# Query norms in a fused attention and feed-forward kernel: four small transfers in place of a TensorE transpose

## The reference

```python
q = (hidden_states @ Wq).reshape(B, Sq, H, D)            # B 4, Sq 512, H 16, D 128
k = (encoder_hidden_states @ Wk).reshape(B, Skv, H, D)
v = (encoder_hidden_states @ Wv).reshape(B, Skv, H, D)
q = rmsnorm(q, gq)                                       # x * rsqrt(mean(x^2) + eps) * g
k = rmsnorm(k, gk)
scores = jnp.einsum('bqhd,bkhd->bhqk', q, k) * scale
attn = jax.nn.softmax(scores, axis=-1)
out = jnp.einsum('bhqk,bkhd->bqhd', attn, v)
return out.reshape(B, Sq, H * D) @ Wo
...
x = x + jnp.tanh(g_xattn[0]) * _L0_xattn_ref(ctx_1024, _layernorm(x), ...)   # selective scan, the mixer
x = x + jnp.tanh(g_ffn[0]) * _L0_ffn_ref(_layernorm(x), ...)                 # quantized feed-forward
x = x + jnp.tanh(g_xattn[1]) * _L1_xattn_ref(_layernorm(x), ctx_1024, ...)   # the attention above
x = x + jnp.tanh(g_ffn[1]) * _L1_ffn_ref(_layernorm(x), ...)                 # four experts
```

## Time and profile before

| | |
|---|---|
| median of 3 runs | 1851.22 us |
| lowest, highest | 1843.35, 1852.04 us |
| time of the profiled execution | 1852.26 us |
| its span, first to last instruction | 1850.5 us |
| busy TensorE, DVE, ScalarE, POOL | 95%, 70%, 52%, 36% of the span |
| mean granted TensorE clock | 0.983 of full |

### The profile page before, as it was taken

How to read it: one execution, slowest core, us unless ns; L and a number is a source line. 1 busy time by engine, 2 the same in 40 slices (tenths; PEclk the granted TensorE clock), 3 DMA queues, 4 the chain that set the end, 5 groups by cost and what they waited for, 6 DMA issues and landing times.

```text
span 1850.5 us, 19507 instructions
## 1 busy us (share of the span) xinstructions
PE 1763.2 (95%) x6114; PEld 809.9 (44%) x6114; DVE 1300.1 (70%) x1899; ACT 963.8 (52%) x1920; POOL 666.5 (36%) x696
## 2 busy tenths in 40 slices
PE   8999899879999999999999999999999899999999
PEld 4333344334444444444444444444444344445543
DVE  4989686989998689899787998987652444422221
ACT  7988786446545546566455566555435334320100
POOL 2434322337463324557222564562223333310000
PEclk9999899979999999999999999999999999999999
DMA  7999833767851146897212589732112799837110
GB/s 262 242 289 286 244 109 116 203 164 187 199 142 57 51 100 162 208 240 200 66 30 74 156 188 251 199 95 69 35 57 91 218 282 293 236 119 273 40 51 28
DMA packets 159045, 292.11 MB, mean 158 GB/s; under 512 B 18424, under 2 KB 51704, under 8 KB 156000
## 3 DMA queue, kind: packets, MB, share of 16 engines
q1 hardware_dynamic: 141664, 227.95, 39.0%
q0 software_dynamic: 17280, 62.92, 17.5%
HBM read 169.51 MB, written 58.26 MB: 123 GB/s over the span
## 4 chain that ended last, share of the span: by engine, by line
PE 72%; DVE 13%; ACT 6%; issue 4%; DMA 3%; POOL 1%; SPq 1%; DVEq 0%; ACTq 0%; POOLq 0%
PE p L846 11%; PE p L806 10%; PE p L823 9%; PE p L857 8%; PE p L893 6%; PE p L697 5%; DVE s_M L1025 5%; PE p L780 4%; PE p L829 4%; PE p L908 3%; PE p L746 3%; PE p L785 3%; DVE s_M L1020 2%; DVE s_M L1032 1%; DVE s_U L1178 1%
## 5 line engine op out<-in xcount | busy, mean ns | idle before, releaser
L1025 DVE TENSOR_TENSOR_SCAN s_M<-s_M 128x1024 f32<-128x1024 f32 x128 | 296.4, 2315 | 9.9 <-ACT s_M L1290 7.6
L1178 DVE CUSTOM_DVE_ANT_0 s_U<-p,s_U 128x512 f32<-128x512 f32 x256 | 188.2, 745 | 161.0 <-PE p L823 159.7
L823 PE MATMUL p<-s_U 128*128 128x512 f32 x512 | 268.2, 612 | 4.6 <-DVE s_U L1178 3.0
L806 PE MATMUL p<-s_U 128*128 128x512 f32 x512 | 256.7, 610 | 3.4 <-ACT s_U L1418 2.7
L1534 POOL DMA_DIRECT2D s_u<-s_M x120 | 111.7, 931 | 383.7 <-DVE s_M L1032 355.6
L1579 POOL TENSOR_SCALAR s_U<-s_U 128x512 f32<-128x512 f32 x256 | 231.9, 926 | 6.3
L857 PE MATMUL p<-s_U 128*128 128x512 f32 x512 | 223.7, 593 | 0.0
L846 PE MATMUL p<-s_U 128*128 128x512 f32 x472 | 216.0, 599 | 2.5 <-ACT s_U L1431 2.4
L1431 ACT COPY s_U<-p 128x512 f32<-128x512 f32 x196 | 105.5, 594 | 176.3 <-PE p L829 175.0
L1290 ACT ACTIVATE s_M<-s_dl,s_small 128x511 f32<-128x511 f32 x256 | 170.3, 717 | 35.5 <-DVE s_M L1025 35.3
L1426 ACT ACTIVATE s_U<-s_U 128x512 f32<-128x512 f32 x256 | 181.6, 710 | 5.3
(11 more groups left out here) (194 smaller groups left out, 2458.3 us busy)
## 6 DMA issues: line engine op xcount, KB each, us to landing
s_u<-s_M POOLq DMA_DIRECT2D x120, 512.0 KB, 7.6
s_bc<-bc_scratch SPq DMA_DIRECT2D x96, 256.0 KB, 4.5
k_scratch<-s_U SPq DMA_DIRECT2D x16, 1024.0 KB, 7.9
v_scratch<-s_U SPq DMA_DIRECT2D x16, 1024.0 KB, 5.4
s_U<-in_Wq SPq DMA_DIRECT2D x64, 256.0 KB, 6.6
s_U<-k_scratch SPq DMA_DIRECT2D x64, 256.0 KB, 5.4
s_U<-rk_scratch SPq DMA_DIRECT2D x64, 256.0 KB, 5.8
s_U<-in_Wo SPq DMA_DIRECT2D x64, 256.0 KB, 4.5
```

The source lines that it names most:

```text
L806: ins = e.matmul(banks[bk][:], wqq[j % 2][:, k, :], axT[b % 2][:, k, :], start=(k == 0), stop=(k == 3))
L823: e.matmul(banks[bk][:], qT[j % 3][:, k * 128:(k + 1) * 128], kT[j % 2], start=True, stop=True).then_inc(S["a_s"], 1)
L1025: e.tensor_tensor_scan(w, dA[i % 2], w, 0.0, ALU.mult, ALU.add).then_inc(S["m_s"], 1)
L1178: e.tensor_tensor_reduce(out=Pm[j % 2][:, k, :], in0=banks[ABANK[kind, j, k]][:], in1=rkb[j % 2], scale=rq[:, k:k + 1], scalar=-3.0e38, op ...
```

## The change

The squares are written in another order: token p of chunk t goes to column 4p + t, not 128t + p. The four matmuls with ones are as before, so partitions 32g to 32g+31 now hold the sums of tokens 32g to 32g+31 of every chunk. One row of each group, cut in 32 pieces of four numbers, is what the partitions 32g to 32g+31 of `rq` need. SP moves it with four transfers, one for each group, to a new semaphore `d_nq`, and POOL's `power` waits for that. The TensorE transpose and the ScalarE copy of step `nt` are gone. ScalarE's next write of `nqs` waits for the transfers of the head before. The planner's cost for `nt` is changed, so the orders of all engines may change.

```diff
-    if x[0] in ("q", "nq", "nt"):
+    if x[0] in ("q", "nq"):
         ABANK[x] = 3
...
-"nt": [("PE", 0.2), ("ACT", 0.3), ("POOL", 1.1)]
+"nt": [("DMA", 2.5), ("POOL", 1.3)]
...
-                    elif kind == "nt":
-                        e.transpose(banks[bk][:, 128:256], nqs[:], identf[:]).then_inc(S["a_nt"], 1)
-                        freed[bk] = (S["a_nqv"], j + 1)
...
-                        e.activation(sq, banks[bk][:], ACT.Square).then_inc(S["a_qs"], 1)
+                        e.activation(sq.rearrange("d (p t) -> d t p", t=4), banks[bk][:].rearrange("d (t p) -> d t p", t=4), ACT.Square).then_inc(S["a_qs"], 1)
                     elif kind == "nq":
                         e.wait_ge(S["a_nq"], j + 1)
                         if j:
-                            e.wait_ge(S["a_nt"], j)
+                            e.wait_ge(S["d_nq"], 64 * j)
                         e.activation(nqs[:], banks[ABANK[kind, j, k]][:, 0:128], ACT.Copy, bias=EPS, scale=1.0 / HD).then_inc(S["a_nqs"], 1)
-                    elif kind == "nt":
-                        e.wait_ge(S["a_nt"], j + 1)
-                        if j >= 3:
-                            e.wait_ge(S["a_mx"], 4 * (j - 3) + 4)
-                        e.copy(rq, banks[ABANK[kind, j, k]][:, 128:256].rearrange("p (t c) -> p t c", c=32)[:, :, 0]).then_inc(S["a_nqv"], 1)
...
                     if kind == "nt":
-                        power(rq, (S["a_nqv"], j + 1), "a_rq")
+                        power(rq, (S["d_nq"], 64 * (j + 1)), "a_rq")
...
+                    elif kind == "nt":
+                        e.wait_ge(S["a_nqs"], j + 1)
+                        if j >= 3:
+                            e.wait_ge(S["a_mx"], 4 * (j - 3) + 4)
+                        for g in range(4):
+                            e.dma_start(head_stats(j)[4][32 * g:32 * g + 32, :],
+                                        nqs[32 * g:32 * g + 1, :].rearrange("o (p t) -> o p t", t=4)).then_inc(S["d_nq"], 16)
```

More of the change, by code:

```diff
@@ L32 @@
 k_k k_v k_n k_kc k_sq k_vc k_nv k_p
-a_s a_q a_nq a_pt a_o a_w a_mx a_m a_nqv a_nqs a_nt a_rc a_x a_qs a_e a_ptc a_oc a_rq a_pd a_tr
+a_s a_q a_nq d_nq a_pt a_o a_w a_mx a_m a_nqs a_rc a_x a_qs a_e a_ptc a_oc a_rq a_pd a_tr
 e_xt e_g e_u e_d e_xc e_s e_rv e_rs e_hn e_it e_y
@@ L355, in context @@
     for kind, j, k in ATTN:
-        does = {"q": [("PE", 0.86)] + ([("ACT", 1.3)] if k == 3 else []), "nq": [("PE", 0.35), ("ACT", 0.4)], "nt": [("PE", 0.2), ("ACT", 0.3), ("POOL", 1.1)], "s": [("PE", 0.86), ("DVE", 0.85)], "ex": [("ACT", 0.9 if k else 1.2)],
+        does = {"q": [("PE", 0.86)] + ([("ACT", 1.3)] if k == 3 else []), "nq": [("PE", 0.35), ("ACT", 0.4)], "nt": [("DMA", 2.5), ("POOL", 1.3)], "s": [("PE", 0.86), ("DVE", 0.85)], "ex": [("ACT", 0.9 if k else 1.2)],
                 "rc": [("POOL", 0.95 if k else 1.3)], "tr": [("DVE", 0.65)], "mv": [("DMA", 2.5)], "mr": [("DMA", 4.0)], "t": [("PE", 0.56), ("ACT", 0.6)], "mx": [("PE", 1.73)], "mix": [("PE", 1.73 if halved("mix", j) else 3.45), ("ACT", 0.6)], "wx": [("PE", 1.73)], "w": [("PE", 1.73 if halved("w", j) else 3.45), ("DVE", 0.8)]}[kind]
```

## The result

The changed kernel takes 1872.22 us in the median of 4 runs (1867.42 to 1873.89); the kernel before, beside it, 1850.37 (4 runs, 1843.35 to 1852.04). The ratio is 1.0121, with a 95% interval of 1.0089 to 1.0153: 22 us slower, where 11 us faster was predicted. The profiled execution took 1867.42 us, its span is 1865.6, the granted clock 0.979 against 0.983.

The account below looks back on a forecast made before the run. TensorE was taken as the bound (72% of the chain). Terms -7.7 - 3.6 - 2.7 + 0 + 1 + 2 = -11.0 us, from 1851.2 to 1840.2, said as 1840 (own range 1836 to 1842; whole range 1828 to 1866).

Parts of the forecast that it names:

- the cover of the landing: GpSimd's power wait, early stretch: norms land 8.8 us after nqs, before the reciprocal is touched; counted as hidden.
- landing beyond the cover: Rival: late small transfers hold GpSimd at power, delaying reciprocal, scaling and TensorE's transposes; 1864 us, slower, chance 0.17.
- +10.4: Early stretch: landing time after nqs, in us, from which the reciprocal is reached and TensorE waits for every further microsecond.
- this is hidden too: Early stretch, accumulating transfer behind power on GpSimd: slips 3.7 us, to 11.3 after issue, inside what already occurs; no cost.
- Hidden as well: Last batch: the reciprocal slips by 2.3 us, but scaling is through 3.9 us before its product is used; no cost.
- Together 6.3 us: TensorE's idle time before the removed transpose (3.6 us) and before the next projection, on the bank-3 copy (2.7 us), goes.
- 64 x 0.12 = 7.7 us: TensorE slots of the 64 removed transposes, 0.12 us each in a dense row, saved; 14.0 us with the idle waits.
- gain given back: Rival: TensorE reaches its next waiting point sooner, half the slots kept and no idle time; 1847 us, same, chance 0.27.
- I take zero: ScalarE's Square with a step of four: no cost taken; upper bound doubled plus 0.57 us, 5.7 us in 10 instances.
- I count nothing: SP's queue: four issues per head fit into SP's waiting time, loads queued behind are for two heads ahead; no cost.
- New stalls: First head without cover, 1 us; feed-forward norm steps behind power on GpSimd, 0 to 14 us, taken as 2.
- Shifted order: Rival: changed planner costs move feed-forward and mixer steps against the heads; 1835 to 1858 us, chance 0.16.

Follow-up runs that it names:

- x4: Changed kernel with power on constants, waiting only for nqs, and the four transfers kept but written to an unused tile; 1854.83 us, ratio 1.0019.
- n1: Changed kernel, GpSimd still waits for the landing, but DVE scales by a constant and waits only for nqs; 1870.02 us, ratio 1.0106.
- n2: Changed kernel with constant norms and GpSimd free of the wait; DVE waits for the landing before a head's first scores; 1854.47 us, ratio 1.0026.
- z1: Changed kernel with old order, constant norms, transfers unread, Square and sums contiguous, two buffers for nqs; 1844.84 us, ratio 0.9976.
- x6: Kernel before with only the Square written at a step of four elements; 1853.34 us, ratio 1.0012.
- x3b: Changed kernel with the Square and its reading by TensorE both contiguous, so norms go to wrong tokens; 1869.01 us, ratio 1.0093.
- y4: Changed kernel with SP issuing the load of Wq behind the four transfers instead of ahead; 1862.73 us, ratio 1.0071.
- x1: Changed kernel with the order of work of the kernel before on all engines but SP; 1876.6 us, ratio 1.0118.
- z4: Changed kernel with the planner's cost for the landing at 8.0 us in place of 2.5; 1859.83 us, ratio 1.0055.
- x3: Changed kernel with the Square contiguous and the sums reading four elements at a step of 128; 1874.4 us, ratio 1.0129.
- y1: Changed kernel with old order, constant norms, transfers unread, one nqs buffer, Square contiguous, sums read at a step of 128; 1857.82 us, ratio 1.0045.
- w2: Changed kernel's order, ScalarE computing the power by logarithm and exponential before the transfers, DVE waiting for the landing; 1979.38 us, ratio 1.0712.

## Why the prediction was wrong

The step that failed is the cover of the landing: "A landing at +8.8 us is 451.4 [...] L1575 is not touched". The wait of GpSimd for the landing was put at nothing, and x4 and n1 against n2 price it at 15 to 19 us. The mechanism of the rival *landing beyond the cover* is what happened, at a chance of 0.17. That its 1864 came within 8 us of the measured time is in part luck: it charged 1 us to each of 24 heads past +10.4, and only 3 of the 48 heads of batches 0 to 2 were past it.

- **The latency was not too low, its spread was left out.** The 8.8 us added two medians of another transfer, 4.2 and 4.6. Measured are 2.8 us for the four issues, 2.8 from the last issue to the last landing, and 6.3 for the whole, all medians over 64 heads. But it goes from 3.6 to 13.0 us, and over 8.8 in 11 of the 48 heads of batches 0 to 2 and in 8 of the 16 of the last batch. One number was held against the cover of one head.
- **The threshold was too high.** "+10.4 us" leaves 1.0 us between the landing and the reciprocal, the time of `power` alone. In head 36 it is 2.9 us, since `power` took 1.7 and an issue of L1526 stands between; in the seven heads of batches 0 to 2 with this pattern it is 2.3 to 3.1. With 2.9, the reciprocal of rows 6, due at +11.4, is reached from +8.5 on, below the 8.8 that the prediction took itself. In the same order of work with and without the wait (the changed kernel and x4), reciprocals come up to 2.1 us later in batches 0 to 2.
- **The accumulating transfers, "this is hidden too".** For their landing that held: DVE waited for it 3.3 us, 6 times, against 1.8 us once. What was missed is their place in GpSimd's queue. The text gave them and the reciprocal each a cover of its own, but one goes behind the other.
- **Last batch, "Hidden as well".** The slip is far larger than the 2.3 us of the text: in eight heads the reciprocal is 2.4 to 6.5 us later than in x4, and DVE waited 27.0 us for L1495 at 5 heads, four of them here. Yet the time nearly bears it: TensorE's idle time there is 10.4 us against 8.8 in x4, and n2, where DVE waits for the landing itself, puts 20.6 us of such waits at about 1 us.
- **"Together 6.3 us", "64 x 0.12 = 7.7 us".** The slots do close: L817 and its copy are gone, TensorE has 64 fewer weight loads. The sum is mis-sized: with no wait at all, z1 shows 4.4 us (1.7 to 7.2 by its interval) where 14.0 were taken; what SP's issues and the traffic may take from it is in this number. It fits the rival *gain given back*, which was not tested by itself.
- **The Square, "I take zero".** It nearly doubled, 1076 ns for 577. That it would be slower is what the rule of the Trainium skill (SBUF — State Buffer, "Door 1: The DMA port swizzle") said, and the trace agrees; by how much it does not say. The bound of 5.7 us held: about 2 us in x6, 3 to 5 us between x3b and the changed kernel, both within the noise.
- **SP's own queue, "I count nothing".** Loads behind the new issues were looked at, what stands ahead of them was not. Wq issued ahead of them cost 9 us (y4), and in head 51 the transfers went out 7.6 us late because SP waited for something else.
- **"New stalls", 1 and 2 us.** No run prices them apart.
- **Shifted order.** x1 puts the old order at the same time as the new, so the orders as such differ by less than its scatter. But an order planned with 8.0 us for the landing wins 12 us (z4): with 2.5 us the planner had placed `power` too early.

Shown is: GpSimd's wait for the landing, with what is queued behind it, makes 15 to 19 of the 22 us. Part of the time goes with a lower granted clock of TensorE (mean over the span, as a share of full): 0.974 to 0.979 in the four runs of the changed kernel, 0.980 to 0.988 in the 19 runs of the kernel before beside y4. What that is worth y4 itself shows, one kernel in ten runs: the five at 0.982 or 0.983 took 1855.7 to 1860.6 us, the five at 0.974 to 0.979 took 1864.9 to 1871.2. So some 7 us of the 22 may show as clock, an estimate from these; whether the clock fell because of the waits is not shown. Open are also the split of the other 3 to 7 us between Square, ScalarE's wait for the old `nqs`, and the lost part of the gain; the share of each piece in GpSimd's queue; the scatter of x1; and why the remedies stop at 1860. The mechanism of before in the new order was not tried.

## What to carry to other kernels

Before a wait moves onto an in-order engine, list what is queued behind it: an engine that is idle for 64% of the time can be the worst place for a wait, and the engine that uses the value the best (n2 against n1). Price the path from the last producer to the last of the transfers, with its issues and with what stands ahead of them in the issuing queue. Hold its spread, not a middle value, against the cover in every place where it is used, and count what must run between the landing and the instruction that is to stay on time. Give a hand-made planner a latency near the measured one first; here that was worth 12 us, where a second queue was worth at most 4 and a second buffer nothing.

## What the runs showed of the hardware

- Four transfers of 0.5 KB each, from SBUF to SBUF, 32 pieces of 16 bytes, took 6.3 us from the data to the waiting engine in the median of 64 heads, 3.6 to 13.0; issuing the four took SP 2.8 us of it in the median, 2.4 to 5.15. One lands in 3.7 us (1.6 to 9.6). The Trainium skill (DMA: Bandwidth & Descriptors, "Anatomy of one DMA — SWDGE (gpsimd) path") has some 2 us of fixed cost for one on GpSimd's path; of these, issued by SP, the fastest took 1.6 us and the median lay well above 2.
- A ScalarE write with a step of four f32 takes 1076 ns for 512 elements, a contiguous one 577; a matmul that reads its moving data four elements at a step of 128, then the next four, takes 422 ns for 128 columns (x3), where it took 273 [in the kernel before, median of L813]. The write changed the time by 2 us in x6; the reading makes 5 us between x3b and x3, and in the old order it is part of y1's 13.
- Logarithm and exponential did not share a loaded table in w2: two loads of 1283 ns for each head. The Trainium skill (ScalarE: Activation LUTs, "Table sets: the hidden batching unit") has both in one set, by which w2 would have had at most one change per head; the trace decides.
- GpSimd's power goes by the element, as the kernel before shows: 1261 ns for 4 per partition, 4049 for 16:

```profile
L1503 POOL TENSOR_TENSOR s_U<-s_U,s_mhalf 128x4 f32<-128x4 f32 x64 | 80.7, 1261 | 136.7 <-ACT s_U L1418 136.0
L1503 POOL TENSOR_TENSOR s_krs<-s_krs,s_mhalf 128x16 f32<-128x16 f32 x16 | 64.8, 4049 | 12.6 <-DMA s_krs<-s_U 12.6
```

The second row is the key norms'. Taken over whole rows of 128 before the transfers it would, by that slope of 232 ns, take some 30 us a head; an estimate, not run.
